# TensorE runs products of constants into an unused bank while it waits in the expert stages and at both ends of the linear attention

## What is computed

```python
x = x + 0.5 * moe0(layernorm(x))      # 8 experts, capacity 256 a expert, relu
x = x + linear_attention(layernorm(x))  # 16 heads of 8, gated state, a scan over 1024 steps
x = x + 0.5 * moe0(layernorm(x))
x = x + 0.5 * moe1(layernorm(x))      # 8 experts, 128 -> 512 -> 128, gelu, no capacity
x = x + softmax_attention(layernorm(x)) # 16 heads of 8, 1024 x 1024 scores
x = x + 0.5 * moe1(layernorm(x))
```

## Time and profile before

| | us |
|---|---|
| median of 3 runs | 877.47 |
| lowest and highest | 875.95, 879.21 |
| the profiled execution | 875.54 |
| its span (first to last instruction) | 873.7 |
| TensorE busy in the span | 670.2 (77%) |
| VectorE busy | 580.2 (66%) |
| ScalarE busy | 454.7 (52%) |
| GpSimd busy | 330.9 (38%) |
| mean granted share of TensorE's clock | 0.881 |

### The profile page before, as it was taken

The page is one execution under the profiler, slowest core; times in us unless marked ns, Lnnn a source line. Parts: engine busy times, 40 slices in busy tenths (PEclk is TensorE's granted clock), DMA queues, the critical chain, the costliest instruction groups (busy, mean ns, idle before and its releaser), DMA issues.

```text
span 873.7 us, 14331 instructions
## 1 busy us (share of the span) xinstructions
PE 670.2 (77%) x4582; PEld 344.9 (39%) x4582; DVE 580.2 (66%) x1141; ACT 454.7 (52%) x872; POOL 330.9 (38%) x767
## 2 busy tenths in 40 slices
PE   4275867645308947799999999999999999951993
PEld 4162322534307944123333434343333423421893
DVE  5426999724633448778787787879978798333343
ACT  2045611224105635047877677867768677851661
POOL 0635564155442432321433324144342444171242
PEclk9996999568558978559999999999999999995897
DMA  8352940035112013620020202020020000011103
GB/s 265 110 147 50 286 69 1 9 110 136 29 40 83 30 55 108 186 66 2 17 40 2 56 1 57 1 57 1 2 56 2 1 2 2 1 37 48 55 29 100
DMA packets 56929, 51.31 MB, mean 59 GB/s; under 512 B 6152, under 2 KB 46804, under 8 KB 56600
## 3 DMA queue, kind: packets, MB, share of 16 engines
q1 hardware_dynamic: 52168, 42.19, 18.4%
q0 software_dynamic: 4544, 7.60, 3.3%
q10 hardware_dynamic: 144, 0.61, 0.2%
HBM read 30.04 MB, written 21.80 MB: 59 GB/s over the span
## 4 chain that ended last, share of the span: by engine, by line
PE 54%; issue 18%; DVE 15%; DMA 5%; SPq 2%; ACT 2%; POOL 2%; another core or an unknown queue 0%; ACTq 0%; POOLq 0%; DVEq 0%
PE PS L1076 14%; PE PS L1004 11%; PE PS L1043 11%; DVE ARENA L1817 6%; PE PS L781 5%; PE PS L792 5%; DVE X L1422 2%; PE PS L744 2%; DMA ARENA<-slots_x 2%; PE PS L753 2%; PE PS L731 2%; DVE XN L1373 2%; DVE STATS L1346 1%; POOL slots_x L1871 1%; SPq L540 1%
## 5 line engine op out<-in xcount | busy, mean ns | idle before, releaser
L1817 DVE TENSOR_REDUCE ARENA<-PS 128x1 f32<-128x1024 f32 x256 | 300.8, 1218 | 62.5 <-PE PS L1004 61.8
L1311 ACT ACTIVATE ARENA<-PS 128x512 f32<-128x512 f32 x512 | 273.0, 607 | 79.0 <-PE PS L1043 73.9
L1004 PE MATMUL PS<-ARENA 72*128 72x512 bf16 x512 | 164.6, 405 | 13.5 <-DMA ARENA<-k_parts 7.1
L1043 PE MATMUL PS<-ARENA 75*128 75x512 bf16 x512 | 162.5, 384 | 1.7 <-issue 1.7
L1076 PE MATMUL PS<-ARENA 128*8 128x128 f32 (+8 forms) x1920 | 151.4, 430 | 1.2 <-POOL ARENA L1993 0.9
L1993 POOL TENSOR_SCALAR_AFFINE_SELECT ARENA<-ARENA 128x128 f32<-128x128 f32 x256 | 73.9, 296 | 127.8 <-ACT ARENA L1311 127.4
L1043 PEld LDWEIGHTS PS<-ARENA 75*128 75x128 bf16 x512 | 47.8, 98 | 90.3 <-ACT ARENA L1311 38.6
L1004 PEld LDWEIGHTS PS<-ARENA 72*128 72x128 bf16 x512 | 42.7, 99 | 98.2 <-DVE ARENA L1817 38.5
L1692 DVE TENSOR_TENSOR ARENA<-PS,ARENA 128x512 f32<-128x512 f32 x46 | 31.8, 692 | 65.5 <-PE PS L781 65.5
L1076 PEld LDWEIGHTS PS<-ARENA 128*32 128x32 f32 (+2 forms) x1920 | 43.2, 97 | 76.8 <-issue 41.7
L1901 POOL DMA_INDIRECT tokens_y<-ARENA x46 | 44.6, 970 | 74.4 <-DVE ARENA L1701 72.3
(11 more groups left out here) (188 smaller groups left out, 878.7 us busy)
## 6 DMA issues: line engine op xcount, KB each, us to landing
ARENA<-pack_dram SPq DMA_DIRECT2D x8, 514.0 KB, 12.7
ARENA<-slots_x SPq DMA_DIRECT2D x16, 256.0 KB, 4.0
slots_y<-ARENA SPq DMA_DIRECT2D x32, 128.0 KB, 2.8
ARENA<-q_parts SPq DMA_DIRECT2D x21, 192.0 KB
ARENA<-k_parts SPq DMA_DIRECT2D x21, 192.0 KB
slots_x<-FILL SPq DMA_DIRECT2D x2, 1483.5 KB, 18.4
ARENA<-slots_x SPq DMA_DIRECT2D x10, 258.0 KB, 5.1
k_parts<-ARENA SPq DMA_DIRECT2D x10, 256.0 KB, 3.7
```

The lines of the kernel that those rows point to most:

```text
L1004: ins = nc.tensor.matmul(PS[:, slot + c, :], Q3[0:KQ, G % Q3R, g, i * P:(i + 1) * P], K3[0:KQ, G % Q3R, g, c * 512:(c + 1) * 512], start=T ...
L1043: nc.tensor.matmul(PS[:, bank, 0:w], K3[0:MR + 3, G % Q3R, i, j * P:(j + 1) * P], Q3[0:MR + 3, G % Q3R, i, half * 512:half * 512 + w], sta ...
L1311: nc.scalar.activation(PT[:, n % NPT, 0:w], PS[:, bank_of[x], 0:w], ACT.Exp).then_inc(b_exp, 1)
L1817: nc.vector.tensor_reduce(NM[:, k % 4, i:i + 1], PS[:, slot:slot + 2, :].rearrange("p b n -> p (b n)"), AX.X, ALU.max, negate=True).then_i ...
```

## The change

A helper `fill(bank, count)` puts `count` products of constants into TensorE's list: the identity as weights, the first 512 columns of the constants as the moving operand, fp32, into a bank that nobody reads at that time. They wait for nothing themselves. They are put ahead of the waits listed in the diff, 146 in all; for three-way tuples the entry is chosen by k. One wait is added: ahead of `last_sums()` TensorE waits for the fifteenth state scan. Nothing else on TensorE and nothing on any other engine is changed. Lines of the changed kernel are 5 to 17 higher.

```diff
+            def fill(bank, count):
+
+                for _ in range(count):
+                    nc.tensor.matmul(PS[:, bank, :], ident, C[:, 0:512], start=True, stop=True)
+
             def norm_turned(ln, kind, k):
...
                 if ln == 5:
 
+                    fill(5, 15)
                     pe.wait_ge(z_scaled, GR)
                     turn(3)
                     logits(3).then_inc(logits_done, 1)
                     counts(k, 1, 3, 0)
+                    fill(5, 19)
                 elif kind in ("ffn0", "ffn1"):
+                    fill(5, (5, 0, 11)[k])
                     turn(0)
+                    fill(5, (1, 1, 9)[k])
                     turn(1)
                     logits(0)
                     logits(1).then_inc(logits_done, 1)
+                    if k == 2:
+                        fill(5, 2)
                     turn(2)
                     if kind == "ffn0":
                         turn(3)
...
                         counts(k, 0, 3, 0)
+                        fill(5, 8)
                         turn(3)
                         logits(2)
                     logits(3).then_inc(logits_done, 1)
                     counts(k, 1, 3, P)
+                    fill(5, (15, 14, 28)[k])
...
+                fill(5, 12)
                 for c in range(2):
                     turn(c)
                     features(2 * c)
...
                 for n in range((B * DH - 1 - SL) // 4 + 1, B * DH // 4 - 1):
                     sums(n)
+                pe.wait_ge(state_done, B * DH - 1)
+                fill(0, 3)
                 last_sums()
+                fill(0, 3)
                 project(1)
```

## The result

| | median, us | lowest to highest, us |
|---|---|---|
| before | 877.81 | 875.95 to 879.21 (6 runs) |
| changed | 905.27 | 900.48 to 911.39 (6 runs) |

The changed kernel is **slower: ratio 1.031, 95% interval 1.028 to 1.035**, 27.5 us. The forecast was 883.5 us with a range up to 890.5, so the sign was right and the size was under a quarter of what came. The profiled execution took 901.55 us, its span is 899.7 us, against 873.7 before: 26.0 us are there to be found in the traces. Three of the six executions of the changed kernel took 900.5 to 901.6 us and three 909.0 to 911.4; the trace is of the first group, and what makes the second 9 us longer isn't known.

The account below looks back on a forecast made before the run. Other engines or DMA bound TensorE's waits, and TensorE at low clock bounds right behind them. Terms 0.1 + 1.0 + 0 - 0.6 + 1.8 + 3.7 = +6.0 us on 875.5, plus 1.9 to the median: 883.5 us, range 873 to 890.5.

Parts of the forecast that it names:

- Step 1: k = 0, head: 5 + 1 products, first logits 0.9 us later, 0.8 given back; net +0.1 us (-0.4 to +1.2).
- Step 2: k = 0, ahead of the slots: 15 products take 15.3 us, 4.0 us late, 3.0 given back; net +1.0 us.
- Step 3: Linear attention's head: 12 products, transposes at 74.4 instead of 71.81, hidden since VectorE takes features only at 82.22; 0.
- Step 4: Linear attention's end: 3 + 3 products cost 0 and keep the clock up into k = 1; -1.1 us (0 to -1.3).
- Step 5: k = 1, ahead of the slots: 14 products take 14.4 us, +1.9, 2.5 given back; with Step 4 net -0.6 us.
- Step 6: k = 2, head: 11 + 9 + 2 + 8 products, first two overruns hidden, second half's logits earlier; -1.9 us.
- Step 7: k = 2, ahead of the slots: 28 products take 24.1 us and outlast the wait; with Step 6 net +1.8 us.
- Step 8: k = 3: rows of 15 and 19 products take 12.9 and 16.3 us, first gelu later; net +3.7 us.
- The products fit the waits: Rival: a product costs about 0.43 us, so no wait is outlasted; 10 to 13 us less, some 866 us; chance 0.13.
- The clock does not stay up: Rival: the clock falls between rows in k = 2 and k = 3; +12 to +14 us, some 890 us; chance 0.12.
- The range's ends (+2.4 and +10): The forecast's sum over the whole kernel, +6.0 us, with every bound at its low end and at its high end.
- a rival of them that went the other way: Waiting inside the first 8 to 9 us of k = 0 and 1 vanishes at high clock; +2.9, 878 to 881 us; chance 0.2.

Follow-up runs that it names:

- all that GpSimd doesn't meet: The changed kernel without the products followed by transposes while GpSimd's gathers or scatters run: 884.35 us against 877.83 for the kernel before, ratio 1.0067.
- the fitting version: The changed kernel without products that GpSimd's transfers meet, with rows cut to fit the waits (20, 10, 14): 874.32 us against 877.83 before, ratio 0.994.
- the 12 products and the pause: Kernel before plus 12 products at the linear attention's head, GpSimd's last eight gathers waiting for ScalarE's first copy: 882.62 us against 880.58, ratio 1.002.

## Why the prediction was right and wrong

**Step 1 (k = 0, head, +0.1).** First logits taken at 17.49 (17.9 said), second counts 0.45 us earlier than before, where +0.1 with a low bound of -0.4 was said. Right within its range, at its end.

**Step 2 (15 products, +1.0).** 14.78 us (15.3 said), 2.7 us late (4.0), give-back 1.3 (3.0, with a low bound of 1.5): at the end of the stage +1.4, where steps 1 and 2 said 1.1. The sum is right by luck: the row was 1.3 us less late than said, and the give-back 1.7 smaller, for here too copies were held (44.28 and 47.12, above).

**Step 3 (12 products, 0).** The step that failed first and most: it put the cost of the 12 products at nothing, and it was +6.3 in the traces, +9 us alone. Its working asked only when TensorE would be done (75.8, with 74.4 said) and how long VectorE could do without it (until 82.22). It took for granted that ScalarE starts its copy at once, as it did behind the first transposes of the kernel before. There TensorE had been idle for 7.47 us, so that row couldn't show it. What shows it is the copy's start set against its transposes'. The name behind the idle time doesn't do it: it is "<-remote" in the changed kernel and "<-issue" in the run of seven products (11.30 us). A sign stood in the kernel before: the prediction says that each wait ends on VectorE's XN or on a DMA, but the 5.85 us at 221.78 are "<-remote", and VectorE had written XN 1.7 us earlier (see the last section).

**Step 4 (3 + 3 products, -1.1).** From the first k v product to k = 1's second counts the changed kernel wins 0.2 us, not 1.1. Within the step's own bounds (0 to -1.3), sized too high: the products did not keep the clock up. Eight transposes of k = 1's head, at 168.55, take 2.35 us, where eight take 1.30 at 16.98.

**Step 5 (k = 1, 14 products).** Products 14.33 us (14.4 said). The size of the row was right and the rest not: +5.0 instead of +0.5 in the stage, +3.9 alone. Same failing as in step 3, beside scatters instead of gathers.

**Step 6 (k = 2, head, -1.9).** Wrong in sign: +3.9 us alone. In the changed kernel the first copy is 22.5 us later than before (238.48 against 215.97, rather than the 12.4 that the stage started late) and the second half's logits 15.0. "The first two overruns are hidden" was true of TensorE's own time, but the copy comes 8.7 us behind the transposes, and no cover reaches that far.

**Step 7 (28 products; with step 6 +1.8).** 25.98 us instead of 24.1, because the granted clock was 0.60 in the mean of its first 4 us. From the second half's logits to the first gelu 33.1 us instead of 27.9 before: +5.3, where the step said 3.7 (its 1.8 and the 1.9 of step 6). The overrun was right, and 1.9 us of it is the cold start that I had priced at 2.4 and put under a rival.

**Step 8 (k = 3, +3.7).** +4.4 in the changed kernel, +4.1 alone. 15 products 13.04 us (12.9 said), 19 products 17.98 (16.3 said): again a cold start. Right, and 0.7 short for it.

**The rivals.** "The products fit the waits" fell by its price: at the full clock the longer rows of products took 0.86 to 0.89 us a product, as the forecast said. "The clock does not stay up" came about at the 28 and at the 19 products, for 1.6 to 1.9 us each, though its price of +12 to +14 did not. The Trainium skill (TensorE: Matmul & The Clock Gate, section "Part 1: The HAM clock gate") says that idleness brings the low clock back; the trace shows that no long wait was needed for it: in the 4.0 us between the 15 and the 19 products TensorE was idle for 2.3 us in all, in pieces of at most 1.7. None of the rivals held a mechanism in which a finished TensorE is not seen to be finished, and this made some 15 of the 20 us that I was short (6.3, 4.5 and about 4 in the three places); cold starts made 2.6. The range's ends (+2.4 and +10) leave out step 4's own bounds; with them they would be +2.2 and +11.2, still far below what came.

**The sum.** Measured alone: 9 (12 products at the linear attention's head), 3.9 (k = 1), 3.9 (k = 2's head), 6 (all that GpSimd doesn't meet), and 1 to 1.4 for k = 0's 15 by the trace: about 24 of 27.5. The missing 3 us are within the intervals of the single runs (over 4 us each way for the first alone), so I can't say whether the holds cost more together.

## What to carry to other kernels

A wait of TensorE may be filled only as far as it reaches: at 0.86 us for an fp32 product of 512 columns the fitting version won 3.5 us by the medians (ratio 0.994), and rows a third to a half longer lost 6. An engine's row of cheap instructions isn't free even where it ends in time: beside a running stream of indirect transfers on GpSimd keep TensorE's rows out, and count instructions rather than time. Stopping the stream took away the hold, but with the 12 products and the pause the kernel was no faster than before (ratio 1.002). A forecast that moves an operation into new company should ask whether any row shows that operation in such company, not only how long it takes.

## What the runs showed of the hardware

**While GpSimd runs indirect transfers, other engines learn of TensorE's work late.** ScalarE's copy, which waits for nothing but the transposes, started over 9 us behind them after 14 records of products; after 24 records with GpSimd's transfers stopped it was 0.64 us. Among the runs at the linear attention's head the delay goes with the number of TensorE's records, not with their length (14 records of 1.7 us held for 9.1 us, 14 of 6.2 us for 9.8, both until the gathers were over), nor with the clock. It is not the same in every execution (six records held in some traces and not in others) nor in every stage (1.8 us after 30 records in k = 0, 5.4 us after 28 in k = 1). That the late thing is the semaphore's update, and not TensorE's work itself, rests on the records, whose ends for TensorE are modelled.

**The kernel before pays some of it too.** k = 1 of the kernel before, TensorE and then ScalarE:

```profile
187.89 1.25 PE L744 MATMUL PS<-ARENA,C 128*128 128x256 f32 x4
```

```profile
190.11 0.47 ACT L1161 ACTIVATE ARENA<-PS,C 128x256 f32<-128x256 f32 x1 [1.39 <-PE PS L744]
192.24 0.47 ACT L1161 ACTIVATE ARENA<-PS,C 128x256 f32<-128x256 f32 x1 [1.66 <-PE PS L744]
```

Both products up are done at 189.1, behind a run of twelve transposes, and GpSimd's last scatter ends at 190.5; the two relus that wait for them start at 190.11 and 192.24. The forecast had seen these gaps ("part of it is waiting whose cause the trace does not name") and made a rival of them that went the other way.

VectorE's word comes late there as well. In k = 2's head of the kernel before, with 4 transposes as TensorE's only work since 208, VectorE writes XN until 220.05:

```profile
218.94 1.11 DVE L1373 TENSOR_SCALAR XN<-X,MV,RSTD 128x128 f32<-128x128 f32 x4 [0.21 <-DVE RSTD L1366]
```

The transposes that wait for it start at 221.78, 1.7 us later, while gathers run until 223.9; at 214.82 they start 0.06 us behind it. So the hold isn't TensorE's alone.

**What stays open** is where the queue is. All times here come from executions in which spans and clock were recorded, so whether the updates are held without a recorder isn't shown. The Trainium skill (NOTIFIC — the notification-queue block, section "7.1 Overflow: three behaviours, one of which stalls the engine") says that the block which writes the trace's records holds back its producers rather than lose a record when its internal pipeline fills; that would fit a queue counted in instructions, and no run here tells it from a queue of the updates themselves.

**The clock fell within 4 us of a full row.** TensorE's granted clock was 1.00 through the 15 products of k = 3 (800.0 to 812.6) and 0.61 from 816.9 to 820.5. In between it ran four transposes, the router products (eight records) and two counts, and was busy for 1.67 us of 4.00.
